# Turning normalised tokens for the projections: from TensorE transposes to VectorE block transposes and SBUF-to-SBUF DMAs

## What is computed

```
x = x + softmax_attention(layernorm(x))      # 2 heads of 128, rotary, causal
x = x + feed_forward(layernorm(x))           # 256 -> 768 -> 256
x = x + linear_attention(layernorm(x))       # 8 heads of 64, with decay and gate
x = x + feed_forward(layernorm(x))           # the same weights
```

## Time and profile before

| what | value |
|---|---|
| device time, median of 3 runs | 2016.64 us (2015.66 to 2017.07) |
| the profiled execution, first to last instruction (its span) | 2018.8 us |
| TensorE, matmuls | 1942.5 us busy, 96% |
| TensorE, weight loads (beside matmuls) | 1678.0 us, 83% |
| VectorE | 1340.9 us, 66% |
| ScalarE | 890.8 us, 44% |
| GpSimd | 335.7 us, 17% |
| mean granted TensorE clock | 0.990 of full |

### The profile page before, as it was taken

How to read it: one execution, slowest core, us unless ns; L and a number is a source line. 1 busy time by engine, 2 the same in 40 slices (tenths; PEclk the granted TensorE clock), 3 DMA queues, 4 the chain that set the end, 5 groups by cost and what they waited for, 6 DMA issues and landing times. The chain is left out here.

```text
span 2018.8 us, 36941 instructions
## 1 busy us (share of the span) xinstructions
PE 1942.5 (96%) x12803; PEld 1678.0 (83%) x12803; DVE 1340.9 (66%) x3222; ACT 890.8 (44%) x1708; POOL 335.7 (17%) x314
## 2 busy tenths in 40 slices
PE   6999999999899999979999999999999999999998
PEld 5888888888688888858888888888888888788887
DVE  5666566656557777756666666666666666677776
ACT  4556555655554444453333333333333333444443
POOL 2112211221100000032222222221222112000000
PEclk9999999999999999989999999999999999899999
DMA  6100000000010000010000000000000000000000
GB/s 221 48 1 0 0 0 0 0 0 0 1 53 0 0 0 0 0 52 1 2 1 1 0 0 0 0 0 0 0 0 0 0 1 1 11 32 31 31 29 34
DMA packets 21983, 27.91 MB, mean 14 GB/s; under 512 B 1057, under 2 KB 20129, under 8 KB 21537
## 3 DMA queue, kind: packets, MB, share of 16 engines
q1 hardware_dynamic: 20800, 24.32, 3.6%
q10 hardware_dynamic: 1120, 2.75, 0.4%
HBM read 18.69 MB, written 8.39 MB: 13 GB/s over the span
## 5 line engine op out<-in xcount | busy, mean ns | idle before, releaser
L818 ACT ACTIVATE ff_silu<-PS 128x512 f32<-128x512 f32 x192 | 115.3, 600 | 290.1 <-PE PS L903 290.1
L865 DVE SCALAR_TENSOR_TENSOR ff_h<-PS,ff_silu 128x512 f32<-128x512 f32 x192 | 132.8, 692 | 125.0 <-PE PS L903 114.0
L1119 ACT ACTIVATE lin_yg_hi<-stage 128x512 fp32r<-128x512 f32 x64 | 40.4, 632 | 384.9 <-DVE stage L1234 373.3
L914 PE MATMUL PS<-ff_w_hi,ff_h_hi 128*128 128x256 f32 x768 | 193.7, 285 | 1.0 <-ACT ff_h_hi L811 1.0
L914 PE MATMUL PS<-ff_w_hi,ff_h_lo 128*128 128x256 f32 x768 | 191.9, 282 | 0.0
L1084 POOL TENSOR_TENSOR lin_yg_lo<-stage,lin_yg_hi 128x512 fp32r<-128x512 f32 x64 | 81.9, 1280 | 577.6 <-ACT lin_yg_hi L1119 577.6
L1196 DVE TENSOR_TENSOR lin_AD<-PS,lin_decay 128x512 f32<-128x512 f32 x128 | 82.1, 682 | 131.5 <-PE PS L1342 131.5
L227 PE MATMUL PS<-ln_xh,lin_w_hi 128*128 128x512 f32 x384 | 152.4, 397 | 15.0 <-DVE lin_w_lo L1165 15.0
L903 PE MATMUL PS<-ln_xh,ff_w_hi 128*128 128x512 f32 x384 | 153.9, 401 | 5.1 <-ACT ff_w_hi L806 2.7
L633 PE MATMUL PS<-probT,v_a 128*128 128x128 f32 x1152 | 154.0, 279 | 4.1 <-DVE oT_lo L495 4.1
L633 PEld LDWEIGHTS PS<-probT,v_a 128*128 128x128 f32 x1152 | 138.9, 192 | 19.3 <-issue 12.7
(11 more groups left out here) (156 smaller groups left out, 4934.2 us busy)
## 6 DMA issues: line engine op xcount, KB each, us to landing
X<-in_x SPq DMA_DIRECT2D x8, 1024.0 KB, 5.3
out_x<-X SPq DMA_DIRECT2D x16, 512.0 KB, 2.9
stage<-in_w_lin SPq DMA_DIRECT2D x1, 2048.0 KB, 7.6
stage<-in_w_gate SPq DMA_DIRECT2D x2, 768.0 KB, 4.3
stage<-in_w_up SPq DMA_DIRECT2D x2, 768.0 KB, 5.8
stage<-in_w_down SPq DMA_DIRECT2D x2, 768.0 KB, 8.1
cos<-in_cos ACTq DMA_DIRECT2D x1, 1024.0 KB, 8.3
qk<-in_w_qkv ACTq DMA_DIRECT2D x1, 768.0 KB, 7.2
```

Source lines behind the costliest of these rows:

```text
L818: nc.scalar.activation(silu[:, f % 2, :], PS[:, 2 + f % 2, :], ACT.Silu, scale=W_SCALE).then_inc(silu_done.sem, 1)
L865: nc.vector.scalar_tensor_tensor(h[:, f % 2, :], PS[:, 4 + f % 2, :], W_SCALE, silu[:, f % 2, :], ALU.mult, ALU.mult).then_inc(h_done.sem, 1)
L914: ins = nc.tensor.matmul(Y[:, t // 2, (t % 2) * M:(t % 2 + 1) * M], a[:, f % NH, t * P:(t + 1) * P], w[:, f % NF, :], start=f == 0 and n = ...
L1119: nc.scalar.activation(yg_hi[:], yg, ACT.Copy).then_inc(yg_hi_done.sem, 1)
```

## The change

Every `Front` (so the groups of both feed-forward phases and of linear attention, not those of softmax attention) is prepared in another way:

- `dve_normalise` writes its result in another order: within a partition by blocks of 32 features, tokens' tiles inside.
- VectorE does one block transpose of 128x1024 into the upper half of `ln_xn` (`dve_blocks`): each block of 32 partitions by 32 elements is turned in itself.
- SyncE moves the blocks to their partitions, 16 DMAs from SBUF to SBUF, each from 32 partitions to 32, in pieces of 32 elements (`sp_move`), into the low part's buffer as plain float32.
- ScalarE takes the high part from there (`act_high`); it waits for all 16 DMAs.
- GpSimd subtracts it in place for the low part (`pool_low`).

In a feed-forward unit: statistics of the group after next in steps 4 and 5; normalise of the next in step 0, block transpose in step 1 behind the residual, the high part at the head of step 4 ahead of its Silu. SyncE waits, before the moves in unit u, until unit u - 1 has made its last up product; stores come behind the moves. In linear attention: the block transpose follows the normalise, the moves wait for the half's last projection, the high part comes ahead of the gated high part of chunk 0, the low part behind the gated low part of chunk 0. In attention: normalise at step 6, block transpose at 7, high part at 13, low part at GpSimd's end.

```diff
+SQ = 32
+NQ = P // SQ
+MOVES = NQ * NQ
+def by_feature_group(buf, t):
+    return buf.rearrange("p t m -> p (t m)").rearrange("p (c k t b) -> p c k t b", c=NQ, k=KT, t=UT)[:, :, :, t, :]
...
             last = nc.vector.tensor_scalar(self.out[:, t, :], ...)
+            if self.by_block:
+                out = by_feature_group(self.out, t)
+                x = x.rearrange("p a (k c b) -> p c (a k) b", k=KT, b=SQ)
...
 class Front:
+    def dve_blocks(self, dve, unit, before=None):
+        dve.wait_ge(self.ln.ready.sem, self.ln.ready.at(unit, 1))
+        if before:
+            front, n = before
+            dve.wait_ge(front.landed.sem, front.landed.at(n, 16 * MOVES))
+        self.nc.vector.transpose(self.blocks.rearrange("p t m -> p (t m)"),
+                                 self.ln.out.rearrange("p t m -> p (t m)")).then_inc(self.blocks_done.sem, 1)
+    def sp_move(self, sp, unit, par):
+        wait_alone(sp, self.blocks_done.sem, self.blocks_done.at(unit, 1), self.sp_passed)
+        lo = self.parts[par][1][:].bitcast(F32)
+        for r in range(NQ):
+            for c in range(NQ):
+                src = self.blocks[r * SQ:(r + 1) * SQ, c, :].rearrange("p (n b) -> p n b", b=SQ)
+                dst = lo[c * SQ:(c + 1) * SQ].rearrange("p k (t r b) -> p (k t) r b", t=UT, r=NQ)[:, :, r, :]
+                sp.dma_start(dst, src).then_inc(self.landed.sem, 16)
+    def act_high(self, act, unit, par):
+        hi, lo = self.parts[par]
+        act.wait_ge(self.landed.sem, self.landed.at(unit, 16 * MOVES))
+        self.nc.scalar.activation(hi[:], lo[:].bitcast(F32), ACT.Copy).then_inc(self.hi_done.sem, 1)
+    def pool_low(self, pool, unit, par):
+        hi, lo = self.parts[par]
+        pool.wait_ge(self.hi_done.sem, self.hi_done.at(unit, 1))
+        self.nc.gpsimd.tensor_tensor(lo[:], lo[:].bitcast(F32), hi[:].bitcast(F32),
+                                     ALU.subtract).then_inc(self.lo_done.sem, 1)
...
@@ feed_forward_phase, SyncE
+                def unit(u, par, first, left):
+                    upcoming = next_of(u, par, left)
+                    if upcoming:
+                        nfront, nu, npar = upcoming
+                        if not first:
+                            wait_alone(sp, up_ready.sem, up_ready.at(u - 1, NF), front.sp_passed)
+                        nfront.sp_move(sp, nu, npar)
...
+                    if not following and not first:
+                        store(u - 1)
@@ feed_forward_phase, ScalarE
                     for f in range(NF):
+                        if f == NF - 2 and upcoming:
+                            nfront, nu, npar = upcoming
+                            nfront.act_high(act, nu, npar)
                         act.wait_ge(gate_ready.sem, gate_ready.at(u, f + 1))
...
-                        if f == NF - 2 and upcoming:
-                            _, _, nsx, nturn = upcoming
-                            nsx.act(act, nturn)
@@ feed_forward_phase, VectorE
-                        if f == NF - 1 and upcoming:
-                            nsx.dve(dve, nturn)
...
-                        if f == 3 and upcoming:
-                            nln.dve_normalise(dve, nln_turn)
...
                         if f == LAG - 1 and not first:
                             residual(u - 1, down_done.at(u, 0))
...
+                        if upcoming and f == 0:
+                            upcoming[0].ln.dve_normalise(dve, upcoming[1])
+                        if upcoming and f == 1:
+                            upcoming[0].dve_blocks(dve, upcoming[1], (front, u))
+                        if after and f == NF - 2:
+                            after[0].dve_tile_stats(dve, after[1], range(UT))
+                        if after and f == NF - 1:
+                            after[0].dve_aggregate(dve, after[1])
@@ feed_forward_phase, TensorE
-                            if f == NF - 2 and upcoming:
-                                _, nln_turn, nsx, nturn = upcoming
-                                nsx.pe(pe, nturn, nln_turn)
@@ linear_attention_phase, SyncE
+                    for half in range(NHALF):
+                        nfront, n = next_of(b, half, last)
+                        wait_alone(sp, proj_ready.sem, proj_ready.at(b, NITEM * (half + 1)), front.sp_passed)
+                        nfront.sp_move(sp, n, 0)
@@ linear_attention_phase, VectorE
+                        nln.dve_normalise(dve, nturn)
+                        nfront.dve_blocks(dve, nturn, (front, b * NHALF + half))
@@ linear_attention_phase, TensorE
-                            elif upcoming:
-                                pe.wait_ge(ad_done.sem, ad_done.at(b, 2 * ch + 2))
-                                upcoming[1].pe(pe, upcoming[2], upcoming[2])
```

More of the change, by code:

```diff
@@ L516, in turn @@
                 def turn(b, first, last):
-                    if last and following:
+                    if last:
                         following.ln.dve_stats(dve, 0)
@@ L757, in run_units, with next_of, after_next @@
         def run_units(eng, unit):
[L760 to L770, removed]
+            unit(0, 0, True, 2)
+            with eng.Fori(0, NU // 2 - 2) as p:
+                unit(p * 2 + 1, 1, False, 2)
+                unit(p * 2 + 2, 0, False, 2)
+            unit(NU - 3, 1, False, 2)
+            unit(NU - 2, 0, False, 1)
+            unit(NU - 1, 1, False, 0)
+        def next_of(u, par, left):
+            if left:
+                return front, u + 1, 1 - par
+            return (following, 0, 0) if following else None
+        def after_next(u, left):
+            if left == 2:
+                return ln, u + 2
+            return (following.ln, 0) if left and following else None
         with nc.Block() as block:
@@ L795, in _, with unit @@
+                def unit(u, par, first, left):
+                    upcoming = next_of(u, par, left)
+                    if upcoming:
+                        nfront, nu, npar = upcoming
+                        nfront.pool_low(pool, nu, npar)
+                    after = after_next(u, left)
+                    if after:
+                        after[0].pool_rstd(pool, after[1])
+                ln.pool_rstd(pool, 1)
+                run_units(pool, unit)
             @block.scalar
             def _(act):
-                sx[1].act_open(act)
@@ L920, in units, with unit @@
                 def units(terms):
-                    def unit(u, par, turn, first, last):
-                        sx[par].pe_wait(pe, turn)
-                        upcoming = next_of(u, par, turn, last)
+                    def unit(u, par, first, left):
+                        front.pe_wait(pe, u)
                         for f in range(NF):
@@ L941, in unit @@
                                 down(u, f - LAG, terms)
-                        if last:
+                        if not left:
                             for f in range(NF - LAG, NF):
@@ L1144, in turn @@
                         for c in range(UT - 1):
[L1145 to L1147 removed]
+                            if c == 0:
+                                nfront, n = next_of(b, half, last)
+                                nfront.act_high(act, n, 0)
                             gated_high(b, UT * half + c)
```

170 lines of the change are left out of this document (87 added, 83 removed).

## The result

| what | before | after |
|---|---|---|
| device time, median | 2016.86 us (4 runs) | 2288.88 us (4 runs, 2287.39 to 2290.22) |
| ratio, with its 95% interval | | 1.1346 (1.1330 to 1.1362) |
| span of the profiled execution | 2018.8 us | 2287.9 us |
| mean granted TensorE clock | 0.990 | 0.923 |

A forecast was written before the change was run, and what follows sets the result against it. TensorE's stream was taken as the bound. Profiled 2018.8 us, plus 214 for 31 feed-forward units (+4.0 wait, +2.9 clock each), minus 15 elsewhere, gave 2218, or 2216 us as median; range 2120 to 2310.

The forecast's parts named there:

- Where this lies in a feed-forward unit: Feed-forward unit: block transpose, sixteen landings, high part, Silu, low part of h; TensorE waits 5.1 us, unit 21.8 against 17.8.
- What is taken away: 384 of 512 TensorE transposes go: 1.04 us per feed-forward unit, 0.87 per linear-attention half, about 1 in attention; 47 us.
- The instructions: Added per group: VectorE block transpose 1.22 us, ScalarE high part 1.04 us, GpSimd low part 2.35 us.
- The price of the DMAs: Sixteen DMAs on SyncE's queue, 0.47 us apart, plus 2.4 us landing: 9.45 us from block transpose to last landing.
- The low part of h, 0.68 us: VectorE's low part of h in a feed-forward unit, taken at 0.68 us, ending at 20.87 us before the down product.
- The clock: TensorE's clock falls after each feed-forward wait; 2.9 us lost per unit, making +6.9 us a unit, 214 us in 31.
- Sum: Whole kernel: 2018.8 + 214 - 15 = 2218 us profiled, 2216 us as the median of runs.
- Linear attention and attention: Outside feed-forward the moves are covered, so 14 us are kept in linear attention and 1 us in attention.
- (a): Rival: the DMAs are hidden in feed-forward units and the kernel is faster, 47 us gained, 1970 us; chance 0.05.
- (b): Rival: TensorE's clock holds in feed-forward units, only +4.0 us per unit, 2126 us; chance 0.17.
- (c): Rival: DMA packets bound at 47 ns each, landing 14.4 us, +11.9 us a feed-forward unit, 2400 us; chance 0.09.
- the straight line between the two rows: DMA packets of 128 bytes, interpolated between 16-byte (9 ns) and 1 KB (47 ns) packets: some 13 ns each.

The follow-up runs named there:

- the last run: Changed kernel with groups normalised and block-transposed a unit earlier, SyncE and GpSimd both issuing moves, low part on VectorE: 1966.73 us, 0.9758 of the kernel before.
- unit_ahead: Changed kernel with feed-forward groups normalised and block-transposed one unit earlier, so moves start with the unit: 1993.92 us, 0.9892 of the kernel before.

## Why the prediction was right, and its size 73 us low

Right were the direction, the place, and the mechanism, in that every link of the chain in **Where this lies in a feed-forward unit** stands in the timeline in that order. The sizes were not right, and of the signs that the prediction named, units of 24 to 25 us, issues 0.4 to 0.5 us apart and an idle time of 5 us all missed (27.3, 0.66 and 8.5). The sum of one unit was 24.7 us (21.8 + 2.9), and measured are 27.3. By its terms:

- **What is taken away: right.** 1.04 us a unit, as the 16.76 us of the last run show, and 1.46 instead of 0.87 in a half of linear attention. Most of the other 0.6 lies at one place: from the next half's first projection to the third run of them, past the last chunk's `y` and output projection, TensorE took 5.17 us before (1239.09 to 1244.26) and 4.63 after (1377.39 to 1382.02). VectorE has as many instructions as before, but its 1.2 us for the group no longer stand in chunk 3; that this is the cause was not tested.
- **The instructions: right.** The block transpose took 1.23 us, 1.22 were taken; the high part 1.06 for 1.04, GpSimd's low part 2.35 for 2.35.
- **The price of the DMAs: the step that failed, in size.** Taken were 0.47 us from one issue to the next, and 2.4 to land: 9.45 us. Measured are (721.05 - 711.20) / 15 = 0.66, the last issue being the end of the row less its own 0.62, and 2.0: 11.95 with the 0.10 from the transpose's end to the first issue. That is 2.5 us a unit, 78 us in 31. The three distances of the earlier trace rows came from loads by the same queue, and even their ends, 0.42 and 0.52, did not hold an SBUF-to-SBUF transfer of 256 pieces. Only the 1.35 of the same rows lay above, and it was left to the range. The runs with eight and four issues show that the issue is paid for each DMA and hardly for its size: 0.61, 0.635, 0.68 us for 32, 64, 128 partitions.
- **The low part of h, 0.68 us: missed.** It takes 1.79 beside GpSimd's low part, 1.1 us a unit in the chain. That GpSimd's instruction was "hidden" was true of TensorE's need for its result and not of VectorE, which works beside it. The Trainium skill, SBUF — State Buffer, section SBUF: two separate sides, has this rule: the two engines share a port pair that one instruction holds to its end, against VectorE's instructions with two inputs in SBUF or in a two-port mode. The traces agree: the low part of h with two SBUF inputs grew by 1.1 us and ended 0.55 us after GpSimd's (727.08 and 726.53, and in the run `unit_ahead` 709.07 and 708.52), while the product at 724.68, which reads PSUM, took its usual 0.69. The normalise, with one such input, was held up too; whether it ran in a two-port mode no trace here shows. The prediction should have weighed this.
- **The clock: too much.** 2.9 us a unit were taken, from slow stretches of 5.4 and 6.1 us of full work. Here the clock fell during the wait, so less work was left in the slow stretch; running without the fall gave back 52 us in 31 units, 1.7 each.
- **Sum:** +2.5 + 1.1 - 1.2 = 2.4 us a unit of the 2.6. Two terms were too low and one too high, so the errors partly cancelled.
- **Linear attention and attention:** -15 was the forecast. The halves gave -21.9. Of the 14.9 us in the joints 13.9 lie where the first units of the two feed-forward phases stand, so they are counted to the 31 units: 276.1 + 13.9 = 290 us against 214 foretold, and -20.9 us against -15 for the rest. The gap in the spans is 76 - 6 = 70 us, 2287.9 against 2218.

That 2289 lies inside the range is in part luck. The bounds given for the issue, 0.42 and 0.52 us, reach to 2239 and did not hold the measured 0.66. The rest of the range stood for two issues of 1.35 us in sixteen and for a block transpose of twice the length. In the unit shown neither happened: sixteen issues took 10.47 us, the transpose 1.23.

**The rivals.** (a) The DMAs hidden, at an issue spacing under 0.23 us, and the time at 1970: excluded by issues of 0.61 us. The 50 ns that the prediction cites beside it, from the Trainium skill, DMA: Bandwidth & Descriptors, Anatomy of one DMA, stand there under the path of GpSimd's DMAs; GpSimd's issue measured 0.58 us. The Trainium skill, DMA: Bandwidth & Descriptors, section Issuing engines are not separate DMA queues, says that a second issuing engine saves the sequencer's time alone, "usually small"; the trace agrees with the first half, and the time saved was 133 us of 2289. (b) The clock holds: it did not, 0.923 in the mean and 0.50 behind the waits of 8.5 us. (c) The packets bound: excluded, since 4096 pieces issued in half the time, or from four DMAs, did not make it slower. The queue over a stretch of 100 us in the first phase, packets, MB, share of 16 engines:

```profile
q1 hardware_dynamic: 15504, 1.87, 11.7%
```

0.117 x 16 x 100 / 15504 = 12 ns for a piece of 128 bytes; the straight line between the two rows gave 13.

## What to carry to other kernels

Count DMAs by their number before their bytes: sixteen small transfers from one queue are a chain of ten microseconds, which hides only if the data are ready a whole unit before they are needed; the same operations were 13% slower or 1% faster than the kernel before by that alone. Work that is "free" on GpSimd has to be laid beside VectorE's program too, since it can stretch an instruction there by more than a microsecond, and where it does is seen by the longest, not by the mean duration of a group. Fewer waits for TensorE pay twice, as its clock was at half speed behind most of them here.

## What the runs showed that was not expected

- An issue of an SBUF-to-SBUF DMA takes 0.61 us on SyncE and 0.58 on GpSimd, each engine on its own account; the loads of the earlier trace rows took 0.38 to 0.47, one 1.30.
- GpSimd's subtraction of 2.4 us lengthens VectorE's low part of h from 0.68 to between 1.79 and 1.89 us, and a normalise of four instructions from 1.38 to 3.54, all of it in the first of the four.
- TensorE's clock falls 2.2 us into a wait of 8.5 us, so that less than half of the slow stretch meets work. Behind waits of 2.25 us it fell in most units and held in some, 20.8 against 19.25 us.
- Neither fix shortened the unit without the other: with the work a unit earlier, two issuing engines or the low part on VectorE left it at 17.54 and 17.1 us, both together brought it to 16.76.
